# Decoder layer on one core: the splits of the next batch's x moved behind k's rotation on GpSimd, two loads later

## The reference

```python
q = (x @ Wq + bq).reshape(B, S, H, D)        # B=4, S=512, H=16, D=32
k = (x @ Wk + bk).reshape(B, S, H, D)
v = (x @ Wv + bv).reshape(B, S, H, D)
q, k = _apply_rope(q, cos, sin), _apply_rope(k, cos, sin)    # x * cos + x_rot * sin
scores = jnp.einsum('bshd,bthd->bhst', q, k) / sqrt(D)       # causal, softmax
out = jnp.einsum('bhst,bthd->bshd', attn, v).reshape(B, S, E)
x = _layernorm(x + out @ Wo + bo)
```

## Time and profile before

| | |
|---|---|
| runs | 987.56 us median (985.23 to 988.04, 3 runs) |
| the profiled execution's own time | 983.27 us |
| its span | 981.5 us |
| busy in the span: TensorE, VectorE, GpSimd, ACT | 931.8, 728.4, 597.2, 514.0 us |
| share of the granted clock over the span | 0.996 |
| GpSimd's x splits (L1480) | 12 of 1.29 us, between 76.5 and 262.8 us |

### The profile page before, as it was taken

One profiled execution on the slowest core, in us unless ns is written; L12 is line 12 of the kernel. 1 busy time (PEld: TensorE's weight loads), 2 busy tenths in 40 slices (PEclk: granted clock), 3 DMA queues, 4 the chain that ended last, 5 costly groups with the idle time before them and its releaser, 6 DMA issues.

```text
span 981.5 us, 16194 instructions
## 1 busy us (share of the span) xinstructions
PE 931.8 (95%) x5272; PEld 754.7 (77%) x5272; DVE 728.4 (74%) x1588; ACT 514.0 (52%) x1150; POOL 597.2 (61%) x645
## 2 busy tenths in 40 slices
PE   7787999999999987998999999999999999999997
PEld 5565877777778765887878888888778878888885
DVE  5566778768877877688777767777777877767767
ACT  4576777767777777557244443333533253333333
POOL 2465745844765646456567775667846776665644
PEclk9999999999999999999999999999999999999998
DMA  6875665966676691002102011111111033011002
GB/s 226 245 197 152 194 161 152 259 158 174 164 203 183 173 280 43 22 38 114 65 0 65 33 65 65 33 65 65 32 34 65 33 108 108 33 65 65 33 33 86
DMA packets 40739, 105.20 MB, mean 107 GB/s; under 512 B 4944, under 2 KB 5072, under 8 KB 38608
## 3 DMA queue, kind: packets, MB, share of 16 engines
q1 hardware_dynamic: 40656, 104.16, 36.0%
HBM read 78.98 MB, written 25.17 MB: 106 GB/s over the span
## 4 chain that ended last, share of the span: by engine, by line
PE 71%; DVE 9%; ACT 8%; POOL 5%; issue 4%; DMA 2%; SPq 1%; POOLq 0%; DVEq 0%; ACTq 0%
PE pd L708 26%; PE pj L656 13%; PE pj L708 9%; PE pg L708 5%; PE pu L708 5%; PE pv L699 4%; PE ps L671 3%; PE pb L684 2%; PE pa L684 2%; ACT prob L898 1%; DVE prob L1161 1%; ACT e L942 1%; ACT raw L888 1%; ACT pT L905 1%; PE ps L656 1%
## 5 line engine op out<-in xcount | busy, mean ns | idle before, releaser
L898 ACT ACTIVATE prob<-prob,nmax 128x512 f32<-128x512 f32 (+3 forms) x256 | 144.0, 563 | 82.0 <-DVE nmax L1161 80.2
L1161 DVE CUSTOM_DVE_ANT_0 prob<-ps,mask 128x512 f32<-128x512 f32 (+3 forms) x256 | 124.6, 489 | 84.0 <-PE ps L671 77.8
L671 PE MATMUL ps<-ks,qs 128*128 128x256 f32 (+2 forms) x256 | 104.6, 410 | 8.1 <-DVE nmax L1161 6.1
L1623 POOL TENSOR_TENSOR g_lo<-gated,g_hi 128x512 fp32r<-128x512 f32 x32 | 49.5, 1546 | 94.3 <-ACT g_hi L1002 94.3
L1456 POOL TENSOR_TENSOR raw<-raw,cos 128x512 f32<-128x512 f32 x32 | 42.3, 1321 | 94.2 <-DVE pj L1143 78.8
L1294 DVE TENSOR_TENSOR xb<-pd,xb 128x512 f32<-128x512 f32 x116 | 79.4, 685 | 26.8 <-PE pd L708 26.7
L1616 POOL TENSOR_TENSOR wop_lo<-wsum,wop_hi 128x512 fp32r<-128x512 f32 x64 | 81.5, 1295 | 1.4 <-ACT wop_hi L987 1.4
L1002 ACT CAST g_hi<-gated 128x512 fp32r<-128x512 f32 x32 | 19.9, 622 | 112.1 <-DVE gated L1354 112.1
L708 PE MATMUL pd<-dn_hi,g_hi 128*128 128x512 f32 x244 | 75.4, 390 | 2.4 <-POOL g_lo L1623 1.1
L708 PE MATMUL pd<-dn_hi,g_lo 128*128 128x512 f32 x244 | 75.2, 389 | 0.0
L708 PE MATMUL pd<-dn_lo,g_hi 128*128 128x512 f32 x244 | 75.1, 389 | 0.0
(11 more groups left out here) (525 smaller groups left out, 2816.7 us busy)
## 6 DMA issues: line engine op xcount, KB each, us to landing
f_raw<-in_w_ffn SPq DMA_DIRECT2D x32, 768.0 KB, 4.2
qs<-qk_scratch SPq DMA_DIRECT2D x64, 256.0 KB, 4.6
ks<-qk_scratch SPq DMA_DIRECT2D x60, 256.0 KB, 7.1
qk_scratch<-qk_hi SPq DMA_DIRECT2D x32, 256.0 KB, 2.0
qk_scratch<-raw SPq DMA_DIRECT2D x32, 256.0 KB, 2.1
res<-in_x SPq DMA_DIRECT2D x4, 1024.0 KB, 4.9
x_scratch<-res SPq DMA_DIRECT2D x4, 1024.0 KB, 5.6
xb<-x_scratch SPq DMA_DIRECT2D x4, 1024.0 KB, 5.9
```

The lines of the kernel that those rows point to most:

```text
L671: pe.matmul(ps[:, t % 2, 0:w], qs[n % 2][:, r, s * P:(s + 1) * P], ks[n % 2][:, r, 0:w], start=True, stop=True).then_inc(s_done, 1)
L898: act.activation(prob[:, t % PROBS, 0:w], prob[:, t % PROBS, 0:w], ACT.Exp, bias=nmax[:, n % 2, i:i + 1], scale=-1.0, accum_out=rsum[:, n ...
L1161: dve.tensor_tensor_reduce(prob[:, t % PROBS, 0:w], ps[:, t % 2, 0:w], mask[:, S - w:S], -D ** -0.5, 3e38, ALU.add, ALU.min, accum_out=nma ...
L1623: pool.tensor_tensor(lo, (gated, gated_b)[b][:], hi.bitcast(F32), ALU.subtract).then_inc((glo_done, glo_b_done)[b], 1)
```

## The change

Two constants. Within a batch, the x tiles 0 and 1 are split in slots 29 and 31 instead of 27 and 28, the tiles 2 and 3 in slots 34 and 36 instead of 34 and 35, on ACT and GpSimd alike. Tiles 2 and 3 are loaded in slots 30 and 32 instead of 28 and 29; tiles 0 and 1 as before.

```diff
 SPLIT_LATE = {(3, 0): 8, ("o", 0): 10, ("o", 1): 12, ("o", 2): 14, ("o", 3): 17}
-LOAD_X = (10, 11, 28, 29)
-SPLIT_X = (27, 28, 34, 35)
+LOAD_X = (10, 11, 30, 32)
+SPLIT_X = (29, 31, 34, 36)
```

## The result

The changed kernel takes 979.22 us, the median of 7 runs (978.3 to 982.2), against 985.23 us for the kernel before on the same chips (983.98 to 988.04, 7 runs). The ratio is 0.9945 with a 95% interval of 0.9929 to 0.996: 5.4 us faster, between 3.9 and 7.0. Timed once more beside one of the experiments it was 0.9963 (0.9951 to 0.9975), which is 3.6 us. The forecast was 4.8 us, and lies between the two.

What follows compares the result with a forecast made beforehand. TensorE, with 71% of the chain, and handovers between engines were taken to bound the kernel. 1.87 + 1.27 + 0.82 + 0.82 = 4.8 us off the 987.56 us median gave 982.8 us, range 979.0 to 988.0.

Steps and rivals of the forecast that it cites:

- The step that carries it, 1.87 us from ACT's chain: First batch: with GpSimd's add earlier, ACT's copy out of `pa` starts at 80.26 instead of 82.13, saving 1.87 us.
- Its first term, 75.61 less 75.42: ACT, first batch: without the split's cast, exp 29 is bound by `nmax` at 75.42, not by 75.61; 0.17 us.
- The later batches, 0.82 us each: Second and third batch: TensorE's idle before the `pa` transposes vanishes, 0.82 us each, bounds 0 and 0.82.
- The clock, 1.27 us: First batch, slot-32 transposes to slot-37 scores: shorter TensorE idle avoids the clock's fall, 1.27 us, bounds 0 to 1.27.
- My sign for it, the full granted clock from 80 to 86 us: Expected in the new profile, first batch: TensorE granted the full clock from 80 to 86 us.
- The loads, costed at nothing with 0.95 us of cover: SP's queue: later loads 2 and 3 cost TensorE nothing; split 3 keeps 0.95 us cover unless load 3 exceeds 3.5 us.
- the signs that I had named: Wrong if `xT_lo` is among TensorE's releasers or an x load exceeds 3.5 us; ACT's load wait about 0.6 us once.
- Rival 3: Load 3 collides with the eight stacking transfers, landing after 8.8 us: 8.9 us slower, 996.5 us; chance 0.05.
- The order on GpSimd and in SP's queue: `split_o` ahead of x split 3 in slot 36 leaves 0.3 to 0.7 us cover; stacking transfers leave no later.
- The sum: All terms together, 4.8 us, taken off the 987.56 us median: 982.8 us; chance 0.50.
- rival 1: The clock falls all the same, or at another place: 3.5 us gained, 984.1 us; chance 0.18.
- Rival 2: Gain goes into the next wait, late `xT_lo` holding TensorE; only ACT's 1.87 us remains: 985.7 us; chance 0.22.

Runs made afterwards that it cites:

- `after_again`: The changed kernel, unaltered, run once more for a second trace; 980.61 us in one run.
- experiments 1 and 3: Kernel before with only load 2, load 3 and split 3 moved: ratio 1.0002; kernel before with three extra GpSimd subtractions ahead of k's add: 1.0041.
- `after_timed`: The changed kernel, unaltered, timed again against the kernel before, beside an experiment with earlier load 3; ratio 0.9963.
- `late_only`: Kernel before with only load 2, load 3 and split 3 moved, splits 0 and 1 left ahead of k's add; 986.09 us, ratio 1.0002.

## Why the prediction was right

**The step that carries it, 1.87 us from ACT's chain.** It was worked out from start-to-start distances, and the time from the scores of slot 28 to the transposes of slot 32 shows it apart from the clock: 10.3 us in all three traces of before, 8.5 in all three of the changed kernel, so 1.8 us. (Its first term, 75.61 less 75.42, is 0.19 and not 0.17; that changes nothing.) ACT became the bound, as said: TensorE's `pa` wait was 1.0 us in `after_again`, and experiments 1 and 3 show that the add's place decides.

**The later batches, 0.82 us each, were 1.00.** The mechanism was right and the size was off. The row's idle counts from the end of the last matmul, but TensorE starts matmuls of 128x512 every 0.23 us while each shows as 0.40 long. The next one could have started 0.17 us before that end. Idle of a pipelined engine is to be read from start to start.

**The clock, 1.27 us.** That the fall belonged to the idle, as I took it, is borne out by seven traces and contradicted by none, but not proved. The price is that of one execution: 0, 1.3 and 2.7 us in three traces of before, 1.3 on average. That the average hit the term is luck; the bounds should have gone beyond 1.27. My sign for it, the full granted clock from 80 to 86 us, is not what the first trace shows: it has the lower level up to 82 us (0.64 from 79 to 82), and `after_timed` too. There it cost nothing: slots 28 to 37 took 12.60 and 12.64 us with it and 12.58 without, in `after_again`.

**The loads, costed at nothing with 0.95 us of cover.** This step was the weakest. By the signs that I had named it even spoke against the forecast: `xT_lo` showed among TensorE's releasers, and a load of x took over 3.5 us. ACT waited 1.39 and 1.74 us for loads and not 0.6 once. The condition was right (it costs from a landing time of 3.5 us on), the landing time was not: I took 2.6 us from a load with nothing beside it, and load 3 took 4.6 us in the first trace, 3.1 in `after_again` and 5.5 in `after_timed`. From slot 37 to 64 this cost 0.9, 0 and 1.8 us. Rival 3 was thus there in part. Its limits are measured too, for the first batch: 3.1 to 5.7 us close ahead of the stacking (5.7 in `late_only`), 8.0 behind it. The 2.0 us of k's low store, which made me give the rival little, was a poor stand-in. The same store took 2.0, 2.5 and 2.6 us in the three traces of before; in the changed kernel, where load 2, k's high store and the low store all left within 1.2 to 2.2 us, it took 5.0, 2.6 and 3.3. So "what is ahead is served first" did not hold, and it wanted a row with the same transfers around it. The section "Issuing engines are not separate DMA queues" of the Trainium skill (DMA: Bandwidth & Descriptors) is borne out as far as transfers interleave. In `late_only` k's two stores ahead of load 3 landed in 2.0 us each, the later by 86.5 us; load 3, issued at 84.82, 0.55 us ahead of the stacking, took 5.7, where load 2 with nothing beside it took 2.6. Most of the slowing so came from what stood behind it, though it is less than in the other order.

**The order on GpSimd and in SP's queue** held. In the changed kernel's second batch split 3 stood behind `split_o` and TensorE did not wait for it, and no wait for the stacking appeared.

**The sum.** By the marks the change brought 4.15 us (1.8 of ACT's chain, 2.0 in the later batches, about 1.3 of the clock, less 0.9 for load 3), the runs say 5.4 and 3.6. Against the marks the forecast of 4.8 is 0.6 too high: it left out the 0.9 for load 3, and the later batches gave 0.4 beyond their term. That these two partly cancel is luck, like the clock's average. The forecast time was 982.8 us and the median is 979.22, only 0.2 above the lower end of the range. Of these 3.6 us, 2.3 are the kernel before: 987.56 was the median of 3 runs, over 7 it is 985.23. Of rival 1, that the clock falls all the same or at another place, the second came in two of three traces of the changed kernel, and cost nothing; one of three executions of before has it too, and against that one there is no clock to win. Rival 2 did not come.

## What to carry to other kernels

On an in-order engine, look at what stands between an operation's inputs and its turn: two splits that nobody needed yet held an add, and behind it an exp, a copy and TensorE. Before an operation is moved, add up the in-order engine that becomes the bound next; here that gave 1.8 us and not the 2.6 us of the wait. A load's landing time is to be taken from one with the same transfers around it, and idle from start to start.

## What the runs showed that was not expected

The same kernel, with the same order of instructions, has its falls of the granted clock at different places. Of three traces of before, two have it with the 2.7 us idle (0.57 and 0.52 granted from 82 to 86 us), the third ahead of it (0.70 and 0.73 from 76 to 82). With the lower level ahead of the idle, the idle itself is 1.56 us and not 2.69, since TensorE spends the time on its slower matmuls instead of standing. A fall in a stretch in which TensorE has time costs nothing: the transposes of slot 32 start 10.29 us after the scores of slot 28 with it and 10.29 and 10.32 without it. And executions differ by 3 us in a part in which no instruction differs (630.3 to 633.3 us from slot 229 to the end), more than half of the effect that was looked for.
